# GpSimd makes two of the eight comparison tiles of each table lookup, VectorE six

## The reference, cut to what matters

```
x = x + _layernorm(attention(_layernorm(x)))        # softmax attention, 16 heads, rope
x = x + _layernorm(ffn_fp4(_layernorm(x)))          # gelu, weights unpacked from 4-bit codes
x = x + _layernorm(linear_attention(_layernorm(x))) # cumulative sums
x = x + _layernorm(ghost_ffn(_layernorm(x)))        # silu, weights looked up in a table
```

```
def _ghost_linear(x, idx, lut):
    w = lut[idx]
    return jnp.einsum('bsh,oh->bso', x, w)
gate = _ghost_linear(x, gate_idx, lut)
up = _ghost_linear(x, up_idx, lut)
h = jax.nn.silu(gate) * up
return _ghost_linear(h, down_idx, lut)
```

## Time and profile before

| | |
|---|---|
| median of 3 runs | 675.18 us (674.12 to 676.3) |
| the profiled execution's own time | 677.76 us |
| its span, first to last instruction | 676.0 us |
| mean granted TensorE clock | 0.948 |
| PE busy | 552.0 us (82%) |
| DVE busy | 537.8 us (80%) |
| ACT busy | 408.7 us (60%) |
| POOL busy | 383.0 us (57%) |

### The profile page before, as it was taken

One profiled execution on the slowest core, in us unless ns is written; L12 is line 12 of the kernel. 1 busy time (PEld: TensorE's weight loads), 2 busy tenths in 40 slices (PEclk: granted clock), 3 DMA queues, 4 the chain that ended last, 5 costly groups with the idle time before them and its releaser, 6 DMA issues.

```text
span 676.0 us, 10925 instructions
## 1 busy us (share of the span) xinstructions
PE 552.0 (82%) x3848; PEld 336.5 (50%) x3848; DVE 537.8 (80%) x1110; ACT 408.7 (60%) x867; POOL 383.0 (57%) x317
## 2 busy tenths in 40 slices
PE   5679998888799998999878899699956878693493
PEld 2246665556466666666644455345524535342252
DVE  7599999989789998998799999884767693676643
ACT  4488888877776688688756573364443454552142
POOL 2699998899988777887647674111441110154021
PEclk9699999999999999999999999989977998996697
DMA  7145554543433566454332220210001000000000
GB/s 258 50 101 124 121 119 113 114 102 75 52 70 77 80 165 89 68 79 79 79 102 94 86 72 3 61 34 9 1 26 37 28 5 1 0 1 0 0 32 31
DMA packets 98390, 44.59 MB, mean 66 GB/s; under 512 B 88224, under 2 KB 90656, under 8 KB 98336
## 3 DMA queue, kind: packets, MB, share of 16 engines
q1 hardware_dynamic: 97344, 43.35, 28.3%
q10 hardware_dynamic: 992, 0.55, 0.3%
HBM read 21.86 MB, written 1.05 MB: 34 GB/s over the span
## 4 chain that ended last, share of the span: by engine, by line
PE 38%; DVE 29%; issue 10%; ACT 9%; POOL 8%; DMA 3%; SPq 2%; POOLq 0%; DVEq 0%; ACTq 0%
PE bank L1293 33%; DVE turned L1121 3%; PE bank L1453 2%; DVE stage L1150 2%; DVE parts L966 2%; DMA pT<-parts 2%; DVE turned L1130 2%; DVE w_all_l L1082 2%; DMA x<-in_x 2%; POOL rr L461 2%; DVE stats L819 1%; POOL rr L460 1%; POOL qkl L468 1%; SPq L377 1%; POOL qkl L490 1%
## 5 line engine op out<-in xcount | busy, mean ns | idle before, releaser
L490 POOL TENSOR_TENSOR qkl<-turned,qkh 128x512 f16<-128x512 f32 (+1 forms) x44 | 55.9, 1270 | 181.0 <-ACT qkh L709 181.0
L1293 PE MATMUL bank<-xTh,w_all_h 128*128 128x512 f16 (+1 forms) x304 | 117.9, 388 | 12.7 <-DVE w_all_l L900 7.7
L1293 PE MATMUL bank<-xTl,w_all_h 128*128 128x512 f16 (+1 forms) x304 | 118.0, 388 | 0.0
L1293 PE MATMUL bank<-xTh,w_all_l 128*128 128x512 f16 (+1 forms) x304 | 117.9, 388 | 0.0
L460 POOL TENSOR_TENSOR rr<-turned 64x512 f32<-64x512 f32 x64 | 82.3, 1286 | 17.2 <-DVE turned L955 12.2
L611 ACT ACTIVATE bank<-bank,nmax 128x128 f32<-128x128 f32 (+3 forms) x128 | 64.0, 500 | 43.7 <-DVE nmax L944 43.3
L468 POOL TENSOR_TENSOR qkl<-rr,qkh 128x512 f16<-128x512 f32 x64 | 73.8, 1157 | 27.4 <-ACT qkh L630 24.9
L709 ACT ACTIVATE qkh<-turned 128x512 f16<-128x512 f32 (+1 forms) x44 | 27.7, 628 | 93.4 <-DVE turned L1130 93.4
L461 POOL TENSOR_TENSOR rr<-turned 64x512 f32<-64x512 f32 x64 | 81.1, 1266 | 3.7
L1130 DVE SCALAR_TENSOR_TENSOR turned<-bank,turned 128x512 f32<-128x512 f32 (+1 forms) x44 | 30.0, 682 | 48.5 <-PE bank L1293 21.2
L966 DVE SCALAR_TENSOR_TENSOR parts<-bank,rscaled,parts 128x128 f16<-128x128 f32 (+3 forms) x128 | 65.5, 547 | 1.1 <-ACT parts L622 1.1
(11 more groups left out here) (189 smaller groups left out, 1555.2 us busy)
## 6 DMA issues: line engine op xcount, KB each, us to landing
stage<-in_per_head SPq DMA_DIRECT2D x16, 512.0 KB, 3.9
xa<-in_codes SPq DMA_DIRECT2D x32, 128.0 KB, 2.7
stage<-in_packed SPq DMA_DIRECT2D x12, 256.0 KB, 3.1
stage<-in_scales SPq DMA_DIRECT2D x12, 256.0 KB, 3.6
pT<-parts SPq DMA_TRANSPOSE x128, 2.8
x<-in_x SPq DMA_DIRECT2D x2, 512.0 KB, 7.1
stage<-in_w1T SPq DMA_DIRECT2D x2, 512.0 KB, 3.7
out<-x SPq DMA_DIRECT2D x2, 512.0 KB, 3.1
```

Of the source, the lines that this page charges most:

```text
L490: pool.tensor_tensor(il[n % 2][0:rows, :], inter[0:rows, n % 2, :], ih[n % 2][0:rows, :], ALU.subtract).then_inc(g_il, 1)
L1293: last = pe.matmul(dst, l, r, start=start and i == 0, stop=stop and i == 2, skip_group_check=skip)
```

## The change

Two of the eight comparison tiles of every lookup, e = 6 and 7, go to POOL in an own function `entries_hit`, with a semaphore g_hot that counts finished lookups of POOL. POOL's part of a lookup waits for the cast indices (d_idx16) and for PE's lookup s-2 (t_lut). It stands in POOL's stream directly behind `low_inter` of the tile whose `product_of` DVE's part follows, ahead of `features`, `numerator` and `low_att` of that tile. DVE's cast now also waits for g_hot of lookup s-2, whose indices it overwrites, and PE's `look_up` for g_hot of its lookup.

```diff
+POOL_ENTRIES = 2
...
+            def entries_hit(s):
+                n = CHUNKS[s // 2][1]
+                pool.wait_ge(d_idx16, s + 1)
+                if s >= 2:
+                    pool.wait_ge(t_lut, s - 1)
+                for e in range(LUT // 2 - POOL_ENTRIES, LUT // 2):
+                    last = pool.tensor_scalar(hot[s % 2][e][:, 0:n], idx16[:, s % 2, 0:n], entry[:, e:e + 1], None, ALU.is_equal)
+                last.then_inc(g_hot, 1)
...
                 if unpack_beside(m):
                     scaled(unpack_beside(m))
+                if m >= M_TILES - 2:
+                    entries_hit(m - (M_TILES - 2))
             for m in range(M_TILES):
                 low_inter(M_TILES + m)
+                for s in lookups_beside(m + 1):
+                    entries_hit(s)
                 if m == 5:
...
                 if s >= 2:
                     dve.wait_ge(d_hot, s - 1)
+                    dve.wait_ge(g_hot, s - 1)
                 dve.tensor_copy(idx16[:, s % 2, 0:n], idx[:, s % 4, 0:n]).then_inc(d_idx16, 1)
...
-                for e in range(LUT // 2):
+                for e in range(LUT // 2 - POOL_ENTRIES):
...
                 pe.wait_ge(d_hot, s + 1)
+                pe.wait_ge(g_hot, s + 1)
                 pe.wait_ge(d_lut, 4)
```

More of the change, by code:

```diff
@@ L203, in sandwich @@
         d_hot = sem("d_hot")
+        g_hot = sem("g_hot")
         t_lut = sem("t_lut")
```

## The result

The changed kernel takes 690.88 us (median of 4 runs, 690.42 to 692.35), the kernel before 675.74 us in the same comparison: a ratio of 1.0217, 95% interval 1.0196 to 1.0238, about 14.7 us slower. The forecast was slower, 684.8 us, 9.6 us over the median before.

The account below looks back on a forecast made before the run. DVE was taken to bound most of the lookup stage. Terms of 0.50 + 1.66 + 2.49 + 0.04 + 1.66 - 0.9 + 4.15 + 0.04 = 9.6 us took the median from 675.2 to 684.8 us, range 674.5 to 695.

Parts of the forecast that it names:

- What goes away: DVE's comparisons: two tiles less save 0.53 us in each of 16 lookups, 9.2 us of work in all.
- What comes back: DVE's comparison stretches: each POOL instruction of length p makes DVE stand still for p less 0.20 us.
- I take p = 0.88: POOL's 512-column comparison: length p estimated at 0.88 us from the select, with 0.52 and 1.15 for the range.
- x: DVE's net extra time per full lookup, 2 (p - 0.20) - 0.53 = 0.83 us, p being POOL's comparison time.
- The new wait of PE: the same cover: PE's wait for POOL's tiles ahead of lookups: costed at nothing, POOL finishing before DVE's third tile from the end.
- The gain of 0.9 us at lookup 10: Lookups 10 and 11: low_att(1) moved behind both lets lookup 10 start earlier, -0.9 us in the sum.
- The lower clock, left out: PE after longer waits at four more places: a lower clock could add up to 1.7 us each, outside the sum.
- The signs named ahead: Profile after: DVE's six tiles 3 to 4 us, waits before lookups 12, 14, 16 up 1 to 2, lookup 10 earlier.
- Costed at nothing and right: DVE's cast waiting for g_hot, covered by queued DVE work; numerator(1) behind lookups 8 and 9, the same 0.9 us.
- the fill price: Rival, chance 0.16: POOL's comparison takes 0.52 us, +0.4 us, 675.6 us, no change.
- truly beside: Rival, chance 0.07: POOL's comparisons don't stop DVE's, so the saving is kept, -5.7 us, 669.5 us.
- The two-input price: Rival, chance 0.27: POOL's comparison is as slow as its subtraction, 1.15 us, +18.3 us, 693.5 us.

Follow-up runs that it names:

- e1: Changed kernel with six DVE tiles per lookup, none on POOL, PE multiplying the first two twice: 670.91 us, 0.992 of the kernel before.
- e2: Changed kernel with POOL's tiles written to a spare buffer, PE not waiting and multiplying the first two tiles twice: 683.5 us, 1.0105 of the kernel before.
- m2: Measuring kernel, no reference computed: 30 DVE comparisons join four POOL instructions already under way; 11.06 us beside POOL comparisons, 8.0 us alone.
- e5: Changed kernel with one comparison tile per lookup on POOL and seven on DVE: 680.15 us, 1.0075 of the kernel before.
- m1: Measuring kernel, no reference computed: POOL instructions alone and beside DVE, which was under way first; POOL comparison 1.56 us alone, two-input subtraction 1.15.
- e4: Changed kernel with POOL's tiles of each pair's first lookup ahead of low_inter in run 2: 685.37 us, 1.0134 of the kernel before.
- e7: Changed kernel, POOL comparing 240 columns into a spare buffer, PE still waiting but multiplying the first two tiles twice: 679.42 us, 1.0049 of the kernel before.
- e8: Kernel before with low_att(1) on POOL one tile later, out of lookup 10: 675.93 us, 1.001 of the kernel before.

## Why the prediction was right or wrong

The sign, and the reason for it, were right: DVE's new total is higher with fewer tiles, because it stands still while POOL works. e1 and e2 show that term alone, 12.5 us against the 5.4 us that the shed tiles are worth. The size was too small by 5 us: PE's wait was put at nothing and measures 7.6 us, while all the rest, 9.6 us in the sum, measures 7.1. That the rest is so near is luck in part, as the third point says. The steps compare as follows.

- **What goes away**: 0.53 us a lookup, 4.8 us on nine lookups or 6.4 on twelve. Right: e1 gained 5.4.
- **What comes back, "p - 0.20"**: wrong as a rule. It was read off POOL's two-input instructions, where it nearly holds (m2: 0.88 for 1.16 us). A comparison on POOL costs DVE about half its length, 0.76 us of 1.56 in m2 and 0.79 in e5. With two in each lookup it was 0.52 on DVE's tiles, or 0.64 with the norm behind a pair: POOL's second pair runs on when DVE's tiles are done (564.60 against 563.12 in the slot shown), beside instructions of which not all are held up. With p = 1.56 the rule would have asked 1.36.
- **The price, "I take p = 0.88"**: wrong, 1.56 us alone and 1.6 to 1.7 beside DVE. The upper bound of 1.15 failed too. It took the two-input subtraction for the dearer one; m1 shows the one-input comparison to be the slower. These two errors work against each other, and that is the luck: the forecast charged DVE 0.88 - 0.20 = 0.68 us for each comparison, and where DVE never idles 0.64 was lost, by a longer instruction and a smaller share of it. So the pairs from 8 on came close to their terms (1.8 us for 1.7, 1.5 a pair for 1.66). Formula and true price together would have given x = 2 x 1.36 - 0.53 = 2.2 us, some 30 us slower; the true hold of 0.52 and the forecast's path give x = 0.51, 12 x 0.51 - 0.9 = 5.2 us, near e2's 7.1.
- **"The new wait of PE: the same cover"**: the step that failed. It was costed at nothing because POOL would finish inside DVE's stretch at p = 0.88. In the changed kernel POOL needs 1.25 + 3.41 us for `low_inter` and its two tiles of the first lookup and is 1.7 us behind DVE; 7.6 us from e2 to the changed kernel. e4 confirms the place: taking `low_inter` out of the way gave back 5.6 us. The price alone isn't what failed here: the cover also leaned on DVE being held for p - 0.20, and in e7, at 0.94 us, POOL was still 0.27 us behind DVE. The prediction named this sign ("over 1.2, or if PE waits for POOL's tile instead of DVE's") but gave it neither a chance nor a price.
- **The gain of 0.9 us at lookup 10**: the distance falls in e2, to 521.88 - 518.73 = 3.15 us, and in e8, where the whole kernel didn't gain by it. In the changed kernel the wait for POOL's tile stands in its place, 4.3 us as before.
- **The lower clock, left out**: it came at lookups 6, 8 and 12 (2.88, 3.52 and 3.06 us for 1.90). Behind 8 and 12 DVE or POOL is what the next step waits for. At lookup 6 it lies on the path: 4.96 us at a granted clock of 0.66 from there to the product behind lookup 7, where the kernel before took 461.21 - 457.92 = 3.29 at 1.00. That is the 1.7 us that the prediction named and left out, and more than the 1.4 us that the stretch up to lookup 7 lost beyond its terms. Why the clock fell at lookup 6, behind 1.96 us of waiting, and not at 14, behind 3.53, stays open.
- **The signs named ahead**: of the forecast's, DVE's six tiles took 3.35 us in the first lookup of a pair, with its busy time up, and the waits ahead of lookups 12 and 16 grew by 2.0 and 1.4 us; the one ahead of 14 did not (3.68 to 3.53), and lookup 10 did not come earlier. Two of the signs of being wrong appeared, POOL's comparison over 1.2 us and PE waiting for POOL's tile.
- **Costed at nothing and right**: DVE's wait for g_hot ahead of its cast. DVE's 16 casts of 512 columns have no idle time ahead of them. `numerator(1)` moved behind lookups 8 and 9 cost what it did before: DVE's product L1162 beside it takes 1.60 us instead of 0.69, and in the kernel before it held up lookup 8 by 3.08 - 2.20 = 0.88 us.

Of the rivals, the fill price and "truly beside" are out: POOL's own price and e1 against e2. The two-input price came nearest in time, 693.5 us, by a p of 1.15 that is as wrong as the forecast's 0.6 to 1.0; no rival had POOL's tile come last. The Trainium skill's sentence that one-input work on GpSimd is roughly line-rate (GPSIMD Engine Reference, section Engine selection) doesn't hold for this instruction: DVE's alone takes 0.265 us, POOL's 1.56. The Trainium skill's rule that the pair of ports is taken for a whole instruction (SBUF — State Buffer, section Who interferes with whom) agrees with the subtraction, 0.88 us for one of 1.16; for the comparison m2 shows DVE let in within it, and the measurement decides.

## What to carry to other kernels

An instruction moved to GpSimd has three prices: what the busy engine sheds, what it stands still for while GpSimd works, and when GpSimd's own share is done, counted from where its queue gets to it. The third is the one to draw as a timeline with the price doubled, since the price of an operation that the trace doesn't show can lie outside what its relatives suggest (here 1.56 us for 0.88). PE's wait then costs only where the busy engine next waits for PE. Before giving work away, look for work on the same engine that merely stands in the wrong order: moving the eight statistics instructions of one norm ahead of one lookup won 2.9 us, where giving away a quarter of the comparisons cost 14.7.

## What the runs showed of the hardware that was not expected

- A one-input comparison or product of 512 columns takes POOL 1.49 to 1.56 us, the two-input subtraction 1.15.
- Beside DVE comparisons, a POOL comparison holds DVE up in two parts of 0.4 us; a subtraction holds it once, for 0.9 us.
- Who is under way first matters: in m1 a row of 20 DVE comparisons that started 0.18 us ahead kept POOL's waiting for 5.0 us and lost nothing itself, while in m2 DVE, joining POOL, lost 0.76 us to each.
- Comparisons of DVE that read PSUM neither slow POOL nor are slowed by it (1.56 us each for POOL, as alone).
